# Ids of six tiles read directly, the block of slot lines in another buffer, ranks in PSUM: a recurrence with routed experts on one core

## What is computed

```python
xn = layernorm(x)                                  # over the last axis
h_t = h_(t-1) * A + xn_t                           # along 2048 tokens, per column
s = h @ BC                                         # 512 x 512
e = argmax(xn @ gate_w.T)                          # one of 8 experts per token
g = silu(xn + xn @ expert_w[e])
out = x + s * g
```

## Time and profile before

| | us |
|---|---|
| runs | 516.45, 516.46, 517.62 |
| median | 516.46 |
| profiled execution | 516.83, of which the span is 515.1 |
| granted clock over the span | 0.991 |

### The profile page before, as it was taken

The page is one execution under the profiler, slowest core; times in us unless marked ns, Lnnn a source line. Parts: engine busy times, 40 slices in busy tenths (PEclk is TensorE's granted clock), DMA queues, the critical chain, the costliest instruction groups (busy, mean ns, idle before and its releaser), DMA issues. The chain is left out here.

```text
span 515.1 us, 10723 instructions
## 1 busy us (share of the span) xinstructions
PE 495.1 (96%) x2739; PEld 388.5 (75%) x2740; DVE 410.1 (80%) x1075; ACT 260.1 (50%) x500; POOL 322.4 (63%) x362
## 2 busy tenths in 40 slices
PE   7999999999999999999988999999999999999993
PEld 6667777777777777777766888888788888887882
DVE  5999899989899989898844777777777777776773
ACT  4676776786687677677422333333333333333330
POOL 2567666666766766766663766656666666646652
PEclk9999999999999999999998999999999999999997
DMA  7978788887877877876245577777777776766620
GB/s 235 350 264 263 222 258 248 246 243 234 271 226 244 271 208 259 257 228 213 104 113 203 185 244 241 237 234 243 234 229 231 230 239 215 231 208 206 216 83 9
DMA packets 65538, 114.27 MB, mean 222 GB/s; under 512 B 9994, under 2 KB 28042, under 8 KB 65504
## 3 DMA queue, kind: packets, MB, share of 16 engines
q1 hardware_dynamic: 47328, 62.46, 39.1%
q0 software_dynamic: 18176, 51.47, 31.7%
HBM read 65.96 MB, written 55.08 MB: 235 GB/s over the span
## 5 line engine op out<-in xcount | busy, mean ns | idle before, releaser
L1073 PE MATMUL ps_s<-w_hi,split 128*128 x284 | 118.3, 417 | 0.1
L643 ACT ACTIVATE ps_s<-ps_s 128x512 f32<-128x512 f32 x71 | 41.3, 582 | 151.5 <-PE ps_s L1075 151.5
L509 POOL DMA_INDIRECT out_dram<-work x71 | 73.2, 1032 | 68.9 <-DVE work L890 59.0
L1074 PE MATMUL ps_s<-w_lo,split 128*128 x284 | 112.6, 396 | 0.0
L1075 PE MATMUL ps_s<-w_hi,split 128*128 x284 | 112.4, 396 | 0.0
L418 POOL TENSOR_TENSOR split<-work,split 128x1024 fp32r<-128x1024 f32 x32 | 77.5, 2421 | 48.6 <-ACT split L571 48.5
L977 PE MATMUL ps_s<-bc_hi,split 128*128 128x512 f32 x256 | 104.1, 407 | 0.7 <-DVE bc_lo L790 0.6
L978 PE MATMUL ps_s<-bc_lo,split 128*128 128x512 f32 x256 | 101.3, 396 | 0.0
L499 POOL DMA_INDIRECT work<-token_rows,work x67 | 69.6, 1038 | 21.7 <-issue 19.8
L436 POOL DMA_INDIRECT slot_table<-token_id,slot_id x64 | 63.0, 984 | 31.6 <-issue 21.1
L685 DVE TENSOR_TENSOR_SCAN work<-a_col,work,ps_xt 128x256 f32<-128x256 f32 x112 | 74.2, 721 | 0.0
(11 more groups left out here) (118 smaller groups left out, 737.9 us busy)
## 6 DMA issues: line engine op xcount, KB each, us to landing
token_rows<-work SPq DMA_DIRECT2D x31, 528.0 KB, 3.2
work<-in_L_attn_inputs_dram SPq DMA_DIRECT2D x31, 512.0 KB, 4.7
token_rows<-work SPq DMA_DIRECT2D x29, 512.0 KB, 5.5
work<-in_L_ffn_expert_w_dram SPq DMA_DIRECT2D x128, 64.0 KB, 4.2
slot_table<-w_lo SPq DMA_DIRECT2D x1, 2080.0 KB, 12.8
token_rows<-in_L_attn_inputs_dram SPq DMA_DIRECT2D x3, 512.0 KB, 10.6
out_dram<-work POOLq DMA_INDIRECT x71, 3.3
work<-token_rows,work POOLq DMA_INDIRECT x67, 4.4
```

Source lines behind the costliest of these rows:

```text
L509: nc.gpsimd.indirect_dma_start(out=out_flat, out_offset=bass.IndirectOffsetOnAxis(ap=slot_tok[:, n:n + 1], axis=0), in_=o_sb[:, u], in_off ...
L1073: nc.tensor.matmul(z_ps[v], hi, wh, start=(k == 0), stop=False)
L1074: nc.tensor.matmul(z_ps[v], hi, wl, start=False, stop=False)
```

## The change

FIRST goes from 4 to 6: the ids of six tiles are read directly, and their scatters take them from ids2 too. ids2 moves from xnt to the low part of the split buffer's first half; the block of slot lines moves from the row buffers to that half's high part; the high and low parts of the second half's tiles all go into the split buffer's other half. first_ids waits for s_done of the group before the last. GpSimd's order of issue becomes ids 0, ids 1, rows 0, ids 2, rows 1, ids 3, rows 2, ids 4, rows 3, block, ids 5, rows 4, rows 5. VectorE casts the block ahead of tile 2 and casts slot_tok behind tile 2; TensorE transposes the slots behind the products of tile 2, and the transposes of tile 1 go into the middle of tile 0's products. Gather 6 and the later ones wait for slot_tok; scatters 0 to 5 don't.

In the last group and the first three, the ranks go into PSUM, where those groups' scores are already. At the last scan, the slot numbers of the group before it are made between its second and third piece, no longer behind it; and ScalarE casts the high part of the last scan ahead of take_s, no longer behind it. RR in the tile loops is called TURN, with the same value.

```diff
-    FIRST = 4
+    FIRST = 6
+    TURN = 6
@@ buffers
-        blk_i = part(FIRST * ROW, P * LINE).bitcast(I32).rearrange("p (q w) -> p q w", w=LINE)
+        blk_i = split[:, 0, 0, 0:P * LINE].bitcast(I32).rearrange("p (q w) -> p q w", w=LINE)
+        ids2 = split[:, 0, 1, 0:FIRST * LINE].bitcast(I32).rearrange("p (j w) -> p j w", w=LINE)
-        x2_hi = [split[:, v, 0, 0:D] for v in range(2)]
-        x2_lo = [split[:, v, 1, 0:D] for v in range(2)]
+        x2_hi = [split[:, 1, v, 0:D] for v in range(2)]
+        x2_lo = [split[:, 1, v, D:2 * D] for v in range(2)]
@@ gpsimd
             def first_ids(j):
+                pool.wait_ge(s_done, TPG * (GROUPS - 1))
                 pool.wait_ge(slot2_ready, 1)
@@ def all_ids
-                pool.wait_ge(lo_done, GROUPS)
@@ def gather
+                wait(pool, o_ready, n - RR + 1)
                 if n < FIRST:
                     pool.wait_ge(ids2_loaded[n], 16)
                     tok = ids2[:, n, 0:1]
                 else:
                     pool.wait_ge(slot_tok_ready, 1)
-                    wait(pool, o_ready, n - RR + 1)
@@ def scatter
-                pool.wait_ge(slot_tok_ready, 1)
+                if n >= FIRST:
+                    pool.wait_ge(slot_tok_ready, 1)
+                tok = ids2[:, n, 0:1] if n < FIRST else slot_tok[:, n:n + 1]
@@ order of issue
-            gather(0, 0)
-            first_ids(2)
+            for c in range(FIRST - 2):
+                gather(0, c)
+                if c < FIRST - 3:
+                    first_ids(c + 2)
             all_ids()
-            gather(0, 1)
-            gather(0, 2)
-            first_ids(3)
-            for c in range(3, RR):
+            first_ids(FIRST - 1)
+            for c in range(FIRST - 2, RR):
                 gather(0, c)
@@ scalar, group
                 if left >= 1:
                     copy_tail(it, c + 1)
                     copy_head(it, c + 1)
+                if left == 1:
+                    high_part(0, c + 1)
                 if not start:
                     take_s(it, c - 1)
                 if start:
                     copy_parts(0, 1)
-                if left >= 1:
+                if left >= 2:
                     high_part(it, c + 1)
@@ vector, scan
                     if k == CH // 2:
+                        if between:
+                            place(it, c - 1, 0)
+                            place(it, c - 1, 1)
                         dve.wait_ge(xnt_tail, n + 1)
@@ vector, route
-                points = bank_score if n < 3 or n == GROUPS - 1 else score
+                points, order = (bank_score, bank_score) if n < 3 or n == GROUPS - 1 else (score, ranked)
@@ (L746, L752 and L759 take order where they took ranked)
@@ vector, second half
             low_x2(0, 0)
-            dve.wait_ge(blk_loaded, 16)
-            nc.vector.tensor_copy(blk_f[0:PLANNED], blk_i[0:PLANNED, :, 0]).then_inc(blk_f_ready, 1)
             normalise(0, 1)
-            dve.wait_ge(slot_turned, 1)
-            nc.vector.tensor_copy(slot_tok[:, :], slot_ps[:, 0:TILES]).then_inc(slot_tok_ready, 1)
             low_x2(0, 1)
             normalise(0, 2)
             for c in range(TILES):
+                if c == 2:
+                    dve.wait_ge(blk_loaded, 16)
+                    nc.vector.tensor_copy(blk_f[0:PLANNED], blk_i[0:PLANNED, :, 0]).then_inc(blk_f_ready, 1)
                 tile(0, c, ahead=TILES - 1 - c)
+                if c == 2:
+                    dve.wait_ge(slot_turned, 1)
+                    nc.vector.tensor_copy(slot_tok[:, :], slot_ps[:, 0:TILES]).then_inc(slot_tok_ready, 1)
@@ tensor, expert
-                    if isinstance(it, int) and it + c == 0 and k == CH - 2:
-                        turn_slots()
+                    if isinstance(it, int) and it + c == 0 and k == CH - 3:
+                        turn_x2(0, 1)
@@ tensor, tiles
-            tile(0, 0, ahead=False)
-            turn_x2(0, 1)
-            for c in range(1, RR):
-                tile(0, c)
+            for c in range(TURN):
+                tile(0, c, ahead=c > 0)
+                if c == 2:
+                    turn_slots()
```

More of the change, by code:

```diff
@@ L51, in bass_recurrent_routed @@
     OR = 3
-    LOOPS = TILES // RR - 1
     PAD = 16
@@ L123, in bass_recurrent_routed @@
         assert plan_at >= at["w"] and plan_at + TILES <= sum(SIZES.values())
-        blk_i = part(FIRST * ROW, P * LINE).bitcast(I32).rearrange("p (q w) -> p q w", w=LINE)
-        assert FIRST * ROW >= 2 * TPG * D
+        blk_i = split[:, 0, 0, 0:P * LINE].bitcast(I32).rearrange("p (q w) -> p q w", w=LINE)
+        assert FIRST >= RR and P * LINE <= CH * GT
         plan = xnt[:, :, :].rearrange("p c n -> p (c n)")
@@ L145, in bass_recurrent_routed @@
         slot2 = sums(6 + 3 * FIRST, 1)[:, 0:FIRST].bitcast(I32)
-        ids2_at = sums_at + (7 + 3 * FIRST) * E
-        ids2 = plan[:, ids2_at:ids2_at + FIRST * LINE].bitcast(I32).rearrange("p (j w) -> p j w", w=LINE)
-        assert ids2_at + FIRST * LINE <= CH * GT and FIRST <= E
-        x2_hi = [split[:, v, 0, 0:D] for v in range(2)]
-        x2_lo = [split[:, v, 1, 0:D] for v in range(2)]
+        pick = sums(7 + 3 * FIRST)[:, 0:4]
+        blk_row = sums(7 + 3 * FIRST)[:, 4:5].bitcast(I32)
+        assert sums_at + (8 + 3 * FIRST) * E <= CH * GT and FIRST <= E
+        ids2 = split[:, 0, 1, 0:FIRST * LINE].bitcast(I32).rearrange("p (j w) -> p j w", w=LINE)
+        x2_hi = [split[:, 1, v, 0:D] for v in range(2)]
+        x2_lo = [split[:, 1, v, D:2 * D] for v in range(2)]
         ident = sb("ident", [P, P], F32)
@@ L506, in scatter @@
                 n = RR * it + c
-                pool.wait_ge(slot_tok_ready, 1)
+                if n >= FIRST:
+                    pool.wait_ge(slot_tok_ready, 1)
+                tok = ids2[:, n, 0:1] if n < FIRST else slot_tok[:, n:n + 1]
                 pool.wait_ge(o_ready, n + 1)
                 nc.gpsimd.indirect_dma_start(
-                    out=out_flat, out_offset=bass.IndirectOffsetOnAxis(ap=slot_tok[:, n:n + 1], axis=0),
+                    out=out_flat, out_offset=bass.IndirectOffsetOnAxis(ap=tok, axis=0),
                     in_=o_sb[:, u], in_offset=None,
@@ L673, in variance, with scan @@
                 last.then_inc(var_ready, 1)
-            def scan(it, c):
+            def scan(it, c, between=False):
                 n = U * it + c
@@ L745, in route @@
                 for t in range(TPG):
-                    last = nc.vector.scalar_tensor_tensor(ranked[:, t], points[:, t], top[:, t:t + 1],
+                    last = nc.vector.scalar_tensor_tensor(order[:, t], points[:, t], top[:, t:t + 1],
                                                           prio[:, t], ALU.is_equal, ALU.mult)
@@ L751, in route @@
                 dve.wait_ge(gate_step, 5 * n + 3)
-                nc.vector.tensor_reduce(first[:, :], ranked[:, :, :], AX.X, ALU.max).then_inc(gate_step, 1)
+                nc.vector.tensor_reduce(first[:, :], order[:, :, :], AX.X, ALU.max).then_inc(gate_step, 1)
                 if ahead:
@@ L758, in route @@
                 for t in range(TPG):
-                    last = nc.vector.tensor_scalar(onehot[:, v, t], ranked[:, t], first[:, t:t + 1], None,
+                    last = nc.vector.tensor_scalar(onehot[:, v, t], order[:, t], first[:, t:t + 1], None,
                                                    ALU.is_equal)
@@ L801, in group @@
                 if left >= 1:
[L802 to L805, removed]
+                    scan(it, c + 1, between=left == 1)
                 if left == 0:
@@ L1053, in turn_x2 @@
                 v = c % 2
-                pe.wait_ge(xn2_ready, RR * it + c + 1)
-                wait(pe, x2_lo_done, RR * it + c - 1)
+                pe.wait_ge(xn2_ready, TURN * it + c + 1)
+                wait(pe, x2_lo_done, TURN * it + c - 1)
                 for k in range(CH):
@@ L1067, in expert @@
                 v = c % 2
-                pe.wait_ge(x2_lo_done, RR * it + c + 1)
-                wait(pe, silu_done, RR * it + c - 1)
+                pe.wait_ge(x2_lo_done, TURN * it + c + 1)
+                wait(pe, silu_done, TURN * it + c - 1)
                 for k in range(CH):
@@ L1089, in _ @@
             stay_busy(6)
-            tile(0, 0, ahead=False)
-            turn_x2(0, 1)
-            for c in range(1, RR):
-                tile(0, c)
-            with pe.Fori(1, LOOPS) as it:
-                for c in range(RR):
+            for c in range(TURN):
+                tile(0, c, ahead=c > 0)
+                if c == 2:
+                    turn_slots()
+            with pe.Fori(1, TILES // TURN - 1) as it:
+                for c in range(TURN):
                     tile(it, c)
-            for c in range(RR * LOOPS, TILES):
+            for c in range(TURN * (TILES // TURN - 1), TILES):
                 tile(0, c, ahead=c + 1 < TILES)
```

4 lines of the change are left out of this document (1 added, 3 removed).

## The result

The changed kernel takes 519.1 us in the median of six runs (518.2 to 520.61), the kernel before 516.11 in six (514.41 to 517.62). The ratio is 1.0062, with a 95% interval of 1.0043 to 1.0081: slower, by 3.2 us (the two medians differ by 3.0). The forecast was 519.9 us, 3.4 more than the 516.46 of before that it started from. The profiled execution took 520.61 us, with a span of 518.9, and is the slowest of the six; the one of before had a span of 515.1.

The account below looks back on a forecast made before the run. TensorE, busy 96% of the span, was taken to bound the kernel. First half -0.16, second half +1.87 and half clock +1.7 summed to +3.4 us on 516.46: 519.9 us, range 516.4 to 520.8.

Parts of the forecast that it names:

- The end of the first half: Last group: PSUM ranks free the one-hot pair from GpSimd, copy_parts comes late, rank products start 0.16 us earlier.
- Nothing waits for that: End of first half: group 30's slot numbers come 1.2 us earlier, freeing GpSimd for its low part, with no effect.
- Tile 0 to 2: Start of second half: first hole and half clock stay, tile 2's transposes (turn 2) come 1.50 us earlier.
- rival (b): Start of second half: no half clock at tile 0 (1.3 us) or copy_parts not late; 516.2 to 516.9 us, chance 0.15.
- The slot transpose: Behind tile 2's products: waits 0.3 us for VectorE's block cast; tile 4's transposes still 1.22 us ahead of before.
- Row 6: Tile 6: gather 6 waits for slot_tok, copied behind residual 2; TensorE idle 2.9 us, turn 6 1.67 us later than before.
- The clock: Behind the hole at tile 6's transposes: TensorE falls to half clock, +1.7 us (bounds 0 and 1.8).
- the last term: The +1.7 us charged to half clock behind the hole at tile 6's transposes.
- no turn waits for them: Behind tile 6: gathers 7 to 10 follow at 2.6 us a tile against 3.23, so they hold up no transposes.
- the sum of +3.4: Whole kernel: +1.87 and -0.16 make +1.7 us, half clock another +1.7; 519.9 us forecast.
- Rival (a): Tile 6: the stall comes without the fall to half clock; +1.7 us, 518.2 us, chance 0.22.
- Rival (c): Tile 6: row 6 is off the path if gather 6 starts by 285.2; 513.8 to 515.4 us, chance 0.10.

Follow-up runs that it names:

- b_psum_ranks: Kernel before with only the ranks of the first three groups and the last put in PSUM, ScalarE's order as before: 516.56 us, ratio 1.0002.
- c_no_psum: Changed kernel with slot_tok one tile earlier, the last scan's cast back behind take_s, and ranks in SBUF again: 514.84 us, ratio 0.9964.
- a_cast_back: Changed kernel with ScalarE's cast of the last scan back behind take_s: 519.01 us, ratio 1.0048.
- a_slots_early: Changed kernel with the block's cast, the slot transpose and the slot_tok copy one tile earlier: 515.29 us, ratio 0.9971.
- a_ids8: Changed kernel with the ids of eight tiles read directly, 6 and 7 behind rows 5: 516.6 us, ratio 0.9991.
- b_turn1: Kernel before with tile 1's transposes behind six products of tile 0 and VectorE's slot_tok copy behind normalise 2: 517.47 us, ratio 1.0016.
- after_again: The changed kernel run once more, nothing altered: 519.8 us, ratio 1.0062 against the kernel before.
- a_fill_hole: Changed kernel with nine products without use ahead of tile 5's products on TensorE: 519.19 us, ratio 1.0045.
- a_slots_mid: Changed kernel with the slot transpose moved behind three products of tile 3 on TensorE, VectorE's order unchanged: 519.65 us, ratio 1.0053.
- a_fill_both: Changed kernel with products without use in both late holes, eight ahead of the slot transpose and nine ahead of tile 5: 520.93 us, ratio 1.0073.
- d_ids8: Changed kernel with eight direct ids, block behind rows 4, slot transpose behind three products of tile 3, last scan's cast behind take_s: 516.74 us, ratio 0.9992.
- c_both: Changed kernel with slot_tok one tile earlier and the last scan's cast back behind take_s: 514.5 us, ratio 0.9964.

## Why the prediction was right, point by point

**The end of the first half: right.** -0.16 us was forecast, -0.15 measured, with the one-hot pair at 0.36 us and copy_parts late as worked out. PSUM does free the pair from GpSimd: 0.36 us inside a low part of 2.41, and the same in b_psum_ranks, where nothing else was changed. The lock itself is in the Trainium skill (SBUF — State Buffer, "Who interferes with whom"); that PSUM rules the two-port mode out, which the forecast cites from there, stands on another of its pages (VectorE: DVE Perf Modes, "Mode 2×_2P — use both read ports for one tensor"). That the ranks in PSUM were worth 0.9 us doesn't hold once the slot numbers are moved too (c_no_psum): the forecast had GpSimd's low part come earlier by that and wrote "Nothing waits for that", but with the ranks in SBUF the pair does.

**Tile 0 to 2: right in mechanism, larger in size.** Without half clock behind the first hole turn 2 came 3.2 us earlier, not 1.5: the 1.5, plus 0.5 of a faster row 0 and the 1.3 that rival (b) had for a clock that holds. In a_cast_back, where the clock did fall there, the hole at turn 2 was the same and turn 2 stood 21.67 us behind the rank products, 1.65 ahead of before: that is the forecast's case and its number. That the clock held in the profile after wasn't forecast; it was rival (b)'s condition.

**The slot transpose: on time, but two terms wrong.** On the clock of the forecast (0.51 us less, by the rank products) row 4 was there at 280.94 (281.0 forecast), the cast ended at 283.60 (283.65) and the slot transpose started at 283.65. So the waiting of 1.79 us, where 0.3 was forecast, is TensorE coming 1.7 us earlier, and the cast not coming with it: VectorE stands 1.48 us ahead of normalise 4 for row 4, gathered at 276.82 and landed 4.6 us later, and residual 1 and the cast are behind that in its order. The forecast had derived the cast from turn 3, a fixed 3.33 us behind it, and with its late turn 3 that gave the right time by luck. In a_cast_back, with the slow clock at the start, the hole was 0.16. The other term is one that the forecast put at nothing: it had turn 4 start where the slot transpose starts, and it starts 0.74 us later, 0.29 for the transpose and 0.45 idle. That is why turn 4 is 0.53 us ahead of before and not 1.22; and what the start wins, row 4 takes.

**Row 6: right.** The gain goes where the forecast put it. Copy of slot_tok, 0.89 us (0.90 forecast), gather, 4.1 us (4.3), normalise 6. The hole was 2.36 us where 2.9 was forecast, because TensorE came later to it; turn 6 was +2.0 where +1.7 was forecast, since the 0.7 us missed at turn 4 made gather 6 0.6 later than forecast, less 0.3 for a faster row. a_slots_early and a_ids8 remove it by different edits and get 4.5 and 3.2 us. This is the step on which the forecast rests, and the experiments bear it out.

**The clock: it fell as said, but it isn't the whole of the last term.** Half clock followed turn 6 in all four profiles that have the stall and nothing in its hole. Its price is as forecast where no row is late behind it: 1.6 us at turn 3 of b_psum_ranks, 1.7 at turn 4 of b_turn1. Behind turn 6 a second wait lies over it that the forecast put at nothing, with "no turn waits for them": gather 7 was issued 2.66 us behind gather 6 and landed 6.0 us later, with scatters 1 and 2 and gather 6 about it on the queue. The transfers held up by one wait are issued back to back once it ends. The two overlap, so what is left to the clock at turn 7 is 0.1 us in the profile after and 1.3 in after_again. From turn 6 to turn 8 the loss grows from 2.0 to 3.9 us in the profile after: 1.5 by turn 7, which either cause would give, and 0.4 more by the low part of tile 6 behind normalise 7.

So the sum of +3.4 held with a last term that is partly right by luck. 1.9 us were charged to row 6 and 1.7 to the clock; measured in the profile after are 2.0 at turn 6 and 1.9 behind it, and there row 7 alone would have given nearly all of the 1.9. In the other executions it is the clock, the row or both; which, the runs don't settle. The range held. Rival (a), the stall without the fall, would have been 518.2: half clock followed turn 6 in both profiles of the changed kernel, and with row 7 late it would have lost more than that behind turn 6. Rival (c) is what a_slots_early makes true: gather 6 started at 284.5 there, against the 285.2 that the forecast named as the point from which it decides, and the kernel was faster.

## What to carry to other kernels

Before a step is moved later on one engine, follow what its result gates on the others, up to the transfer and its landing: here the copy of a small table, put behind tile 2, held GpSimd for 7 us and queued up three transfers behind the gather. A hole that is closed is worth nothing if a wait that runs on its own time stands behind it, so sum the absolute time of the last wait, not the holes. When two edits act on the same wait, take one away again; here either did all of it. When two waits overlap, look at a second execution of the same kernel before one of them is called the cause; here the profile after and after_again name different ones.

## What was not expected of the hardware

**Holes of equal length, with and without half clock.** The hole ahead of turn 0 was 1.94 to 1.99 us in seven profiles (before, a_fill_hole, a_cast_back, a_slots_mid, b_psum_ranks, a_fill_both, a_ids8). Half clock followed in three of them (before, a_cast_back, b_psum_ranks) and not in four. A single profile therefore doesn't tell whether a hole of 2 us costs 1.7 us more.

**ScalarE standing with its input ready.** In four profiles (c_no_psum, d_ids8, a_ids8, a_fill_both) ScalarE stands 3.4 to 4.4 us ahead of its first silu, where the others have 0.9 or less, and the silu comes 2.6 to 3.6 us late. Its rows in d_ids8:

```profile
277.82 0.58 ACT L644 ACTIVATE ps_s<-ps_s 128x512 f32<-128x512 f32 x1 [4.32 <-remote]
280.69 0.59 ACT L639 CAST split<-ps_xt 128x512 fp32r<-128x512 f32 x1 [2.29 <-remote]
```

and the same silu in c_both, whose ScalarE program is that of c_no_psum:

```profile
274.36 0.58 ACT L644 ACTIVATE ps_s<-ps_s 128x512 f32<-128x512 f32 x1 [0.81 <-PE ps_s L1078]
```

In c_no_psum the transfer of instructions (queue q8 of the profile) that falls in this stretch lies between 276.0 and 276.5, and the silu starts at 277.09; in c_both one at 276.5 to 277.0 is there too, but the silu had run already. That ScalarE waited for its code behind the gathers fits, and isn't shown: nothing here moves that transfer. There is a rival that no run separates: the four are exactly the profiles taken on chip 6, and none of the eight others whose chip is known (2 and 7) has it, so it may hang on the chip or on that set of runs and not on the kernels. The times of these four may carry it too. In d_ids8 it put a hole of 3.55 us ahead of tile 2's products, so that kernel's design isn't judged by its profile.

**A short hole behind the slot transpose.** Wherever the slot transpose stands with a wait between two tiles, 0.45 to 0.47 us follow in which TensorE is idle though normalise 4 is done (five profiles). It is gone where the transpose is inside a tile. Between the two stands the load of the expert's number into a register; that this is what is then waited for is argued, not tried.
